# Moving one addition of the value stage from GpSimd to VectorE in a fused attention and filter kernel

## What is computed

```
x1 = x + L0(_gn(x))
A  = Wa xh + ba ;  Bm = Wb xh + bb ;  V = Wv xh + bv       (per head, 64 x 64 weights)
attn_maps = softmax(Bm, positions) ;  attn_vecs = softmax(V, channels)
G  = A attn_maps^T ;  Z = G attn_vecs                       (L0's result)
```

## Time and profile before

| | us |
|---|---|
| median of 3 runs | 16896.57 |
| lowest and highest of them | 16895.24, 16900.56 |
| the profiled execution's own time | 16895.63 |
| span of its trace | 16893.9 |
| mean granted clock of TensorE | 0.968 |

### The profile page before, as it was taken

How to read it: one execution, slowest core, us unless ns; L and a number is a source line. 1 busy time by engine, 2 the same in 40 slices (tenths; PEclk the granted TensorE clock), 3 DMA queues, 4 the chain that set the end, 5 groups by cost and what they waited for, 6 DMA issues and landing times.

```text
span 16893.9 us, 444493 instructions
## 1 busy us (share of the span) xinstructions
PE 15309.3 (91%) x140452; PEld 12527.2 (74%) x140452; DVE 12971.0 (77%) x27498; ACT 11149.8 (66%) x19714; POOL 6884.2 (41%) x11797
## 2 busy tenths in 40 slices
PE   7999989999889998998989999899998999989999
PEld 5777777777777777777777777777777777777777
DVE  7777777777777777778777787777877778777787
ACT  5666666666666666666666666666666666666666
POOL 4433444434444344443444434444344443444434
PEclk9999999999999999999999999999999999999999
DMA  2122111221111211112111121111211112111120
GB/s 65 42 55 61 45 40 42 55 61 47 42 42 52 61 48 41 42 53 59 50 42 41 51 58 52 41 42 50 58 54 41 41 48 58 56 40 42 47 58 21
DMA packets 1147389, 819.66 MB, mean 49 GB/s; under 512 B 32068, under 2 KB 1080644, under 8 KB 1146308
## 3 DMA queue, kind: packets, MB, share of 16 engines
q1 hardware_dynamic: 1146308, 805.84, 17.1%
HBM read 537.30 MB, written 268.44 MB: 48 GB/s over the span
## 4 chain that ended last, share of the span: by engine, by line
PE 41%; DVE 32%; issue 15%; ACT 7%; DVEq 3%; POOL 1%; ACTq 0%; POOLq 0%; SPq 0%; DMA 0%
PE ps L902 41%; DVE t L812 4%; DVE nrun L690 4%; ACT yb L532 4%; DVE yb L852 3%; DVE nblk L686 3%; DVE z L818 3%; DVE sth L744 3%; DVE xn L805 2%; DVE mrun L675 1%; DVE xh L827 1%; DVE yr L840 1%; DVE srun L674 1%; DVE stc L574 1%; DVE yr L842 1%
## 5 line engine op out<-in xcount | busy, mean ns | idle before, releaser
L418 POOL TENSOR_SCALAR yb<-yb 128x512 f32<-128x512 f32 x4096 | 2543.1, 621 | 6590.7 <-DVE yb L852 6590.7
L532 ACT ACTIVATE yb<-ps,bias_b 128x532 f32<-128x532 f32 x4096 | 2885.2, 704 | 2966.8 <-PE ps L902 2641.0
L902 PE MATMUL ps<-dn_t,yb 128*128 128x64 f32 (+1 forms) x32768 | 4465.8, 272 | 90.4 <-DVE z L818 53.1
L902 PEld LDWEIGHTS ps<-dn_t,yb 128*128 128x128 f32 x32768 | 4116.3, 191 | 337.8 <-DVE z L818 198.4
L852 DVE SCALAR_TENSOR_TENSOR yb<-yb 128x532 f32<-128x532 f32 x4096 | 2889.6, 705 | 1697.8 <-ACT yb L532 1692.2
L902 PE MATMUL ps<-up,t 128*128 128x266 f16 x24576 | 3465.1, 276 | 0.0
L902 PE MATMUL ps<-up,xn 128*128 128x266 f16 x12288 | 2107.1, 284 | 585.5 <-DVE t L812 387.8
L902 PEld LDWEIGHTS ps<-up,t 128*128 128x128 f16 x24576 | 2337.7, 102 | 286.5
L902 PEld LDWEIGHTS ps<-up,xn 128*128 128x128 f16 x12288 | 1061.8, 101 | 1205.7 <-DVE t L812 705.5
L407 POOL TENSOR_TENSOR xh<-xh,pt 128x512 f32 (+1 forms) x1024 | 1685.8, 1646 | 578.4 <-DVE pt L725 578.4
L398 POOL COPY xn<-xh 128x512 f32 x1024 | 1095.3, 1072 | 2002.6 <-PE ps L902 1338.2
(11 more groups left out here) (146 smaller groups left out, 25446.7 us busy)
## 6 DMA issues: line engine op xcount, KB each, us to landing
xc<-in_x SPq DMA_DIRECT2D x512, 512.0 KB, 5.8
xh<-in_x SPq DMA_DIRECT2D x480, 512.0 KB, 6.4
out<-xh SPq DMA_DIRECT2D x480, 512.0 KB, 3.7
xh<-in_x SPq DMA_DIRECT2D x64, 256.0 KB, 3.4
out<-xh SPq DMA_DIRECT2D x64, 256.0 KB, 3.0
bias_b<-in_bias SPq DMA_DIRECT2D x1, 256.0 KB
bias_r<-in_bias SPq DMA_DIRECT2D x10, 2.0 KB
wa<-in_WaT SPq DMA_DIRECT2D x2, 16.0 KB
```

The costliest lines, as they stand in the source:

```text
L418: nc.gpsimd.tensor_scalar(v[:, :, 0:2 * P], v[:, :, 0:2 * P], CLAMP, -CLAMP, ALU.min, ALU.max).then_inc(s_yc, 1)
L532: act.activation(yb[:, i % YRING, :, :], y_ps[i % 2], ACT.Identity, scale=UPGAIN * GAIN, bias=bias_b[:, bass.ds(c0 + i, 1)]).then_inc(s_y, 1)
L902: return nc.tensor.matmul(o, l, r, start=start, stop=stop, skip_group_check=share)
```

## The change

`add_z` is taken from POOL and put on DVE, directly behind `norm_z` of the same block. DVE waits on its own `s_zs` before it. POOL's loop now only spreads the maximum. The wait for `s_x1` at the head of `norm_z` is gone with the credit: the additions and the normalisations are now in the order of one engine. The operation itself, its operands and their access patterns stay as they are.

```diff
@@ -401,12 +400,6 @@
-            def add_z(u, k, par):
-                wait_alone(pool, s_zs, NBLK * u + k + 1 + ZCREDIT)
-                xv = xh_wc[:, bass.ts(k, WB), :]
-                nc.gpsimd.tensor_tensor(xv, xv, zs_[par][:].rearrange("p w h m -> p w (h m)"), ALU.add).then_inc(s_x1, 1)
-
-            pool.sem_inc(s_x1, XCREDIT)
             pool.sem_inc(s_yq, YRING)
@@ -427,14 +420,9 @@
-                for par in range(2):
-                    spread(u, par, par)
-                with pool.Fori(1, NBLK // 2) as k:
+                with pool.Fori(0, NBLK // 2) as k:
                     for par in range(2):
                         spread(u, 2 * k + par, par)
-                        add_z(u, 2 * k + par - 2, par)
-                for par in range(2):
-                    add_z(u, NBLK - 2 + par, par)
@@ -716,7 +704,6 @@
                 def norm_z(k, par):
                     bb = NBLK * u + k
-                    dve.wait_ge(s_x1, bb + 1)
                     dve.wait_ge(s_zz, bb + 1)
@@ -724,6 +711,12 @@
+                def add_z(k, par):
+                    dve.wait_ge(s_zs, NBLK * u + k + 1 + ZCREDIT)
+                    xv = xh_wc[:, bass.ts(k, WB), :]
+                    nc.vector.tensor_tensor(xv, xv, zs_[par][:].rearrange("p w h m -> p w (h m)"),
+                                            ALU.add).then_inc(s_x1, 1)
@@ -733,11 +726,13 @@
                     if before(2):
                         norm_z(k - 2, par)
+                        add_z(k - 2, par)
                 steps(dve, NBLK, RING, max_v)
-                norm_z(NBLK - 2, 0)
-                norm_z(NBLK - 1, 1)
-                wait_alone(dve, s_x1, NBLK * (u + 1) + XCREDIT)
+                for k in range(2):
+                    norm_z(NBLK - 2 + k, k)
+                    add_z(NBLK - 2 + k, k)
+                wait_alone(dve, s_x1, NBLK * (u + 1))
```

More of the change, by code:

```diff
@@ L246, in attention_then_filters @@
         MCREDIT = 2
-        XCREDIT = 2
         SCREDIT = 2
```

## The result

The changed kernel takes **17090.08 us** (median of 4 runs, 17086.90 to 17094.75) against 16896.48 of before (4 runs, 16895.24 to 16900.56): a ratio of 1.0114, 95% interval 1.0101 to 1.0127. It is slower by 194 us, 1.1%. The forecast was 16876 and no change; the range reached to 17100 and holds the result, but the sign was wrong.

A forecast was written before the change was run, and what follows sets the result against it. PE's beat of 2.676 us a block was taken to bound the value-stage loop, POOL only the stage's end. Loop nothing, end 20.5 us gained: 16895.6 - 20.5 = 16875.1, or 16876 against the median; range 16858 to 17100.

The forecast's parts named there:

- What bounds the kernel: Value stage: PE works without a gap, 2.676 us a block; POOL is on the path only at the stage's end.
- 1.48 + A: DVE's length of a block in the value-stage loop, in us, against PE's 2.676; A is the addition's duration.
- A: Duration of one addition on DVE, taken as 1.15 us; over 1.20 us DVE becomes the bound.
- Step (c): Addition on DVE: source and result streams step together and overlap nearly whole, so it takes 1.15 us.
- Rival 2: Value-stage loop: result's stepping half exposed, addition 1.37 us, block 0.174 us over the beat; 17039 us, 12 in 100.
- Step (b): DVE's loop gains 1024 additions; each starts 0.03 us behind its normalisation, and DVE's block stays under PE's beat.
- Step (a): POOL loses 1024 additions of 1.65 us; worth nothing in the loop, and removing credit and wait costs nothing.
- Rival 3: Value-stage loop: the addition waits 0.14 us for POOL's late spread, both using SBUF; 16960 us, 6 in 100.
- Step (d): End of the value stage, last normalisation to statistics: 1.96 us becomes 1.32, gaining 0.64 us a unit, 20.5 in all.
- The second figure under rival 2: Addition time by the skill page's 2.50 ns for a stepping result: an estimate of 1.42 us, time near 17090 us.

The follow-up runs named there:

- e1: Kernel after with the addition's computed address replaced by a constant, so sums go to wrong columns: 17020.77 us, ratio 1.0073.
- e2: Kernel after with fixed addresses and four forms of the addition: source and result stepping, only source, only result, neither; 16915.64 us in one execution.
- e9: As e2, but source and result alike at steps of 2, 4 or 24 floats, or in pairs with a hop of 4: 16900.89 us, one execution.
- e12: Kernel after with one once-only POOL operation, 26 unread PE matmuls a unit, and z reordered so the addition meets runs of 4 floats: 16775.77 us, ratio 0.9927.
- e5: Kernel after with one more POOL operation, a column multiplied by 1.0 once before the unit loop: 17069.18 us, ratio 1.0104.
- e4: Kernel after with the addition of block k-3 put behind the maximum of block k, before the normalisation of k-2: 16922.76 us, ratio 1.0015.
- e8: Kernel before with only the last of a unit's 32 additions moved to DVE, plus one once-only POOL operation: 16895.64 us, ratio 1.0001.
- e10: Kernel before with 26 matmuls a unit that nobody reads, put where PE idles: 16812.67 us, ratio 0.9951.

## Why the prediction was wrong

- *What bounds the kernel* held: PE's beat of 2.676 us in the loop, POOL at the stage's end alone. So did the limit: DVE's block is 1.48 + A, and over A = 1.20 DVE is the bound. With A = 1.30 it gives 2.78; e1 measured 2.777.
- *Step (c), the size of A,* is **the step that failed**. I let the stepping result hide behind the stepping source and took 1.15 us; it measured 1.30, over the limit of 1.20. On DVE one stream costs 0.36, less than ACT's 0.465, but the second adds 0.27 (e2). Rival 2 (half exposed) had this mechanism. It is 90 of the 194 us.
- *What the Trainium skill says to this.* The Trainium skill's "Vector Engine (DVE) Microarchitecture Reference", section 5.2, names 1.98 ns a column for all three streams leaving their neighbourhood at every element, and 2.50 for both sources, or the result alone, at a step of 24 words. For one source and the result, e2 gives 1.04 ns + (1.320 - 0.692) us/512 = 2.27 ns at 128 words, and e9 2.49 at 24. The same section of the Trainium skill says that a port keeps its full rate only while its elements come in runs of at least two adjacent words. The pairs of e9 and the runs of four of e12 agree (0.69 us); a step of 2 floats, which is no pair, was free as well, and there the measurement decides.
- *Step (b), the gap behind the normalisation,* failed as well: I took 0.03 us from the wait behind the reciprocal. The normalisation behind that wait has no address to compute. The addition has, and it costs 0.11 us more in 24 blocks of 32: 84 us (e1). This term was missing. With A = 1.30 and without it my sum gives 28 x 0.104 - 0.49 = 2.4 us a unit, about 16973, still 117 under the measured time. The trace before had shown such a cost, on POOL: its additions in the loop, with `FUSED_REGOPS` ahead of them, started 0.27 or 0.40 us behind the normalisation, and the last two of a unit, without, 0.19.
- *Step (a), POOL's relief costs nothing:* wrong in a place I did not look at. The addition carried POOL's reconfiguration; without it the filter stage pays 0.92 us a unit in its rest. Taking it out was worth 21 us in the kernel after (e5).
- *Rival 3, DVE and POOL holding each other up:* not at the spread, as computed (it starts 0.17 us behind the maximum throughout and is over before the addition starts), but real at line 789, and in e4 from the other side. The reaction of 0.40 us that I feared for the spread belongs to additions with a computed address and the reconfiguration ahead of them; the spread has neither.
- *Step (d), the end of the stage:* 0.50 us a unit with A = 1.30, where the same sum gives 0.49. But it was not 16 us of the total in e8, where the clock took it back.
- *The range* (16858 to 17100) holds 17090 by luck. Its upper end stood over rival 2, which needed A = 1.37 and came to 17039; the measured time lies higher, with a smaller A, because of two terms that no case had. The second figure under rival 2, A = 1.42 and near 17090, meets the time by the same luck: A is 1.30.

The sum in us over 32 units, from the table: addition 90, address 84, rest of the filters 29 (the reconfiguration), first 31 filter matmuls 19, less 22 for the end (0.18 + 0.51 a unit), less 5 for the other stretches, makes 195. No run isolates the 19; in the trace the granted clock is at 0.50 for 4.8 us of that stretch where it was 3.9 before.

## What to carry to other kernels

Before an operation moves to an engine that has 0.05 us of room in its beat, price its access pattern from both streams, and add what the engine's queue has to do: an address computed behind a wait is paid in full (0.11 us here). Write a strided addition so that at least two neighbours follow each other, by changing the order in which its producer writes (e12). And when an operation leaves an engine, compare the queue's own instructions of all stages, not only of the one that was edited.

## What the runs showed of the hardware

- DVE, 128x512 float32, source and result in step: 0.69 us contiguous, at a step of 2 floats, and in pairs or runs of four; 1.13 at 4 floats, 1.44 at 24, 1.32 at 128. Stepping by 256 floats in PSUM: nothing.
- A DVE operation whose address is computed in the loop started 0.15 us behind the end of the operation it waited for, and 0.03 with a fixed address (after, e1).
- A DVE operation with two SBUF sources and a POOL operation that reads SBUF hold each other up, whichever comes second: 0.25 to 0.40 us for DVE's single column, 0.62 to 1.46 for POOL's copy.
- MODIFY_POOL_CONFIG shows as 11 ns, and the clip behind it started 0.15 us later.
- TensorE's granted clock was 0.50 from 164 to 170 us of the kernel before, behind a stretch of 8 us in which PE was busy for 5.5, and again from 256 to 268, where PE was busy for 2.1; it was still at 0.50 when the matmuls returned. Filling PE's idle time there was worth 83 us (e10).
